# Moving the roundings, the bias and the rectifier of a feed-forward between ScalarE and VectorE

## The reference, cut to what matters

```python
q_mul = lambda x: _float_quantize(x, 5, 2)
q_acc = lambda x: _float_quantize(x, 5, 10)
def _qlinear(x, W, b):
    y = q_acc(jnp.einsum('bsk,nk->bsn', q_mul(x), q_mul(W)))
    return q_acc(y + q_mul(b))
h = jax.nn.relu(_qlinear(x, W1, b1))      # 96 -> 384
y = _qlinear(h, W2, b2)                   # 384 -> 96
# used as  t = t + ffn(layernorm(t))
```

## Time and profile before

| | |
|---|---|
| median of three executions | 7506.49 us |
| the profiled execution | 7508.82 us |
| its span in the profile | 7506.7 us |
| `ffn2`, from its first load's issue to that of the next phase | 6957.2 to 7128.1 us |
| `ffn3`, from its first load's issue to the end | 7335.3 to 7506.7 us |
| DVE, ACT, POOL busy over the whole span | 6432.9, 5446.9, 5465.7 us |

### The profile page before, as it was taken

How to read it: one execution, slowest core, us unless ns; L and a number is a source line. 1 busy time by engine, 2 the same in 40 slices (tenths; PEclk the granted TensorE clock), 3 DMA queues, 4 the chain that set the end, 5 groups by cost and what they waited for, 6 DMA issues and landing times. The chain is left out here.

```text
span 7506.7 us, 105881 instructions
## 1 busy us (share of the span) xinstructions
PE 6068.7 (81%) x18336; PEld 2113.4 (28%) x18336; DVE 6432.9 (86%) x7490; ACT 5446.9 (73%) x11128; POOL 5465.7 (73%) x4289
## 2 busy tenths in 40 slices
PE   7888888888888872888888888888887768798696
PEld 2222222222222220222222222222222113498252
DVE  6999999999999995499999999999999985533636
ACT  7888888888888873577777778777777764322757
POOL 5888888888888881488898898888888871000606
PEclk8999999889989986888999999999999888997898
DMA  4445445445445445587888888888877773346222
GB/s 101 108 104 117 107 106 116 107 108 115 106 106 116 106 101 143 115 186 182 186 187 185 187 189 186 185 188 187 187 183 186 184 165 92 124 137 195 81 57 77
DMA packets 584349, 1050.60 MB, mean 140 GB/s; under 512 B 105735, under 2 KB 140732, under 8 KB 579100
## 3 DMA queue, kind: packets, MB, share of 16 engines
q1 hardware_dynamic: 584060, 1047.70, 58.7%
HBM read 857.89 MB, written 189.54 MB: 140 GB/s over the span
## 5 line engine op out<-in xcount | busy, mean ns | idle before, releaser
L1644 POOL TENSOR_TENSOR scan_prod<-scan_hs,scan_BC_rep 128x512 f32<-128x512 f32 x1536 | 1943.8, 1273 | 312.8 <-DVE scan_hs L1568 303.8
L664 POOL TENSOR_TENSOR mamba_prod<-mamba_hs,mamba_BC_rep 128x512 f32<-128x512 f32 x1536 | 1919.7, 1274 | 216.6 <-DVE mamba_hs L621 214.8
L621 DVE TENSOR_TENSOR_SCAN mamba_hs<-mamba_dA,mamba_carry,mamba_dbx 128x512 f32<-128x512 f32 x1152 | 1425.3, 1265 | 1.6
L1193 PE MATMUL scan_u_rep<-scan_du,scan_sel 96*128 96x512 f32 x1536 | 935.2, 693 | 538.7 <-DVE scan_hs L1568 538.5
L546 ACT ACTIVATE mamba_dA<-mamba_delta_rep,mamba_a_neg 128x512 f32<-128x512 f32 x1536 | 1092.5, 712 | 121.5 <-DVE mamba_hs L621 118.8
L1418 ACT ACTIVATE scan_dA<-scan_delta_rep,scan_a_neg 128x512 f32<-128x512 f32 x1536 | 1092.3, 712 | 96.1 <-DVE scan_hs L1568 84.7
L1568 DVE TENSOR_TENSOR_SCAN scan_hs<-scan_dA,scan_carry,scan_dbx_even 128x512 f32<-128x512 f32 x768 | 975.8, 1271 | 45.6 <-ACT scan_carry L1398 27.9
L1568 DVE TENSOR_TENSOR_SCAN scan_hs<-scan_dA,scan_carry,scan_u_rep 128x512 f32<-128x512 f32 x768 | 976.3, 1271 | 40.8 <-ACT scan_carry L1398 36.7
L600 DVE TENSOR_TENSOR mamba_dbx<-mamba_u_rep,mamba_BC_rep 128x512 f32<-128x512 f32 x1152 | 776.7, 674 | 88.1 <-PE mamba_u_rep L332 75.6
L1967 POOL TENSOR_TENSOR ffn_sq<-ffn_xm 96x512 f32<-96x512 f32 x64 | 66.3, 1036 | 954.4 <-DVE ffn_xm L1935 943.3
L332 PE MATMUL mamba_u_rep<-mamba_du,mamba_sel 96*128 96x512 f32 x768 | 466.5, 692 | 317.4 <-DVE mamba_hs L621 316.9
(11 more groups left out here) (286 smaller groups left out, 10776.8 us busy)
## 6 DMA issues: line engine op xcount, KB each, us to landing
scan_BC_rep<-proj_rows SPq DMA_DIRECT2D x1024, 256.0 KB, 6.4
scan_delta_rep<-proj_rows SPq DMA_DIRECT2D x1024, 192.0 KB, 3.6
mamba_BC_rep<-bc_units SPq DMA_DIRECT2D x512, 256.0 KB, 8.1
mamba_delta_rep<-delta_units SPq DMA_DIRECT2D x512, 192.0 KB, 3.7
proj_rows<-scan_dbc SPq DMA_DIRECT2D x256, 224.0 KB, 3.4
delta_units<-mamba_delta SPq DMA_DIRECT2D x128, 192.0 KB, 5.8
by_n<-fin_res SPq DMA_DIRECT2D x32, 768.0 KB, 3.2
fmid_src<-by_n SPq DMA_DIRECT2D x32, 768.0 KB, 5.2
```

Source lines behind the costliest of these rows:

```text
L621: nc.vector.tensor_tensor_scan(hs[:, s % RING_H], dA[:, s % RING_A], dbx_bank(s)[:], carry[:, bass.ds(at, 1)], op0=ALU.mult, op1=ALU.add). ...
L664: pool.tensor_tensor(prod[:, (G * u + s) % RING_P], hs[:, s % RING_H], BC_rep[:, u, QUADS + s % QUADS], ALU.mult).then_inc(s_prod, 1)
L1193: nc.tensor.matmul(u_rep[c][:], sel[:, c], du[:, k], start=True, stop=True).then_inc(s_rep_u, 1)
L1644: pool.tensor_tensor(prod[:, (G * k + s) % RING_P], hs[:, (G * k + s) % RING_H], BC_rep[:, k, 2 + s % 2], ALU.mult).then_inc(s_prod, 1)
```

## The change

ScalarE's `relu` and `add_bias` go to VectorE, and VectorE's `round_sums` goes to ScalarE. ScalarE then reads both products out of PSUM; VectorE adds the biases, and the maximum with zero, with `tensor_scalar` from 16-bit SBUF tiles to 16-bit SBUF tiles. The wait for the bias tiles moves to VectorE with them. The lags stay; `relu` precedes `narrow` in VectorE's step, and `add_bias` is its last part.

```diff
-            def relu(n):
-                wait(act, s_h8, n - 1)
+            def round_sums(n):
                 for j in range(J):
-                    act.wait_ge(s_sum, J * n + j + 1)
-                    nc.scalar.activation(act16[:, n % 2, j], sum16[:, n % 2, j], ACT.Relu, bias=b1f[:, j:j + 1]
-                                         ).then_inc(s_act, 1)
+                    k = J * n + j
+                    act.wait_ge(s_hid, k + 1)
+                    wait(act, s_act, k - 2 * J + 1)
+                    nc.scalar.activation(sum16[:, n % 2, j], hid[k % HB][:], ACT.Copy).then_inc(s_sum, 1)
...
-            def add_bias(n):
-                act.wait_ge(s_o16, n + 1)
-                wait(act, s_res, n - 1)
-                nc.scalar.activation(y16[:, n % 2], out16[:, n % 2], ACT.Identity, bias=b2f[:]).then_inc(s_y16, 1)
-
             nc.scalar.preload_act_table_set(EXP_LN)
-            act.wait_ge(s_bq, 2)
             act.wait_ge(s_set, 2)
-            staggered(((4, log), (11, round_out), (5, rsqrt), (8, relu), (12, add_bias)))
+            staggered(((4, log), (11, round_out), (5, rsqrt), (7, round_sums)))
...
-            def round_sums(n):
+            def relu(n):
+                wait(dve, s_h8, n - 1)
                 for j in range(J):
-                    k = J * n + j
-                    dve.wait_ge(s_hid, k + 1)
-                    wait(dve, s_act, k - 2 * J + 1)
-                    nc.vector.tensor_copy(sum16[:, n % 2, j], hid[k % HB][:]).then_inc(s_sum, 1)
+                    dve.wait_ge(s_sum, J * n + j + 1)
+                    nc.vector.tensor_scalar(act16[:, n % 2, j], sum16[:, n % 2, j], b1f[:, j:j + 1], 0.0, ALU.add, ALU.max
+                                            ).then_inc(s_act, 1)
+
+            def add_bias(n):
+                dve.wait_ge(s_o16, n + 1)
+                wait(dve, s_res, n - 1)
+                nc.vector.tensor_scalar(y16[:, n % 2], out16[:, n % 2], b2f[:], None, ALU.add).then_inc(s_y16, 1)
...
-            staggered(((0, centre), (7, round_sums), (9, narrow)))
+            dve.wait_ge(s_bq, 2)
+            staggered(((0, centre), (8, relu), (9, narrow), (12, add_bias)))
```

## The result

The changed kernel takes 7540.49 us (median of 5 runs, 7532.7 to 7546.34) against 7502.77 for the kernel before (5 runs beside it, 7494.86 to 7511.48): a ratio of 1.0047, 95% interval 1.0034 to 1.006. The forecast was 7538 in a range of 7504 to 7571, slower by 31.6 us. The two medians differ by 37.7, the two profiled spans, 7544.5 and 7506.7, by 37.8.

The account below looks back on a forecast made before the run. POOL's 4.05 us middle step, its own work plus waiting in turns with VectorE's SBUF casts, was taken as the bound. 2 x (17.0 in the middle - 1.2 at the ends) = +31.6 us on 7506.5 gave 7538, range 7504 to 7571.

Parts of the forecast that it names:

- That the new instructions take turns: Feed-forward phases: VectorE's four new SBUF-to-SBUF instructions a unit alternate with POOL's, as the narrowing cast does; four turns more.
- The size of the step: Middle of both feed-forward phases: 4.90 us a step, the middle of two orders of turns, 0.85 over 4.05.
- order (a): Middle step: POOL, already waiting, wins after every VectorE instruction, and its next add waits for VectorE's bias; 4.94 us.
- order (b): Middle step: VectorE keeps its turn and POOL loses all five of VectorE's instructions in a row; 4.85 us.
- The add's new wait: Middle step: POOL's next add may start only after VectorE's bias, last in its step; included in 4.94 us.
- The number of middle steps: Middle of each phase: twenty steps, each 0.85 us longer, +17.0 us a phase.
- The filling: Four or five steps before unit 0's add in each phase: 0, with 1 us to either side.
- The ends: Last steps of each phase, without squares: 13.06 us become 11.84, a gain of 1.2 a phase; the last adds cancel.
- 1: Rival on the new VectorE instructions: they stream like 8-bit casts, 0.42 us each; +64 us, 7570 us; chance 0.13.
- 2: Rival on the new VectorE instructions: one element a cycle and no turns; +20 us, 7527 us; chance 0.08.
- 3: Rival: new instructions fast without turns, POOL keeps 4.05, ScalarE's relief shows at the ends; -14 us, 7493 us; chance 0.12.
- 4: Rival: TensorE's clock falls, a quarter of the 40 steps taking 7.0 us; 21 us more, 7559 us; chance 0.07.

Follow-up runs that it names:

- relu_psum: Kernel before with rectifiers on VectorE reading straight from PSUM, rounding of hidden sums left out, bias left on ScalarE: 7506.6 us against 7509.16, step 4.11.
- idle_psum: Changed kernel plus one useless VectorE cast of 256 columns out of PSUM per step, ahead of `centre`: 7569.23 us in one run, step 4.89.
- idle_sbuf: Changed kernel plus one useless VectorE copy of 512 columns between 16-bit SBUF tiles per step, behind `centre`: 7566.60 us in one run, step 5.16.
- bias_first: Changed kernel with the output's bias directly behind `centre` in VectorE's step: 7542.05 us in one run against 7515.94 for the kernel before, step 4.76.
- pe_order: Changed kernel with TensorE's hidden products issued ahead of the variance: 7564.25 us in one run beside 7524.40 for the kernel before, step 4.88.
- square_act_pe: Changed kernel with POOL's squares on ScalarE, a third x8 buffer and hidden products ahead of the variance: 7521.37 us in one run, step 4.21.
- square_act: Changed kernel with the square moved from POOL to ScalarE: 7514.0 us against 7509.16 for the kernel before, ratio 1.0007, step 4.09.
- relu_only: Changed kernel with the output's bias left on ScalarE, only the rectifiers on VectorE: 7531.88 us against 7509.16 for the kernel before, ratio 1.0032, step 4.56.

## Why the prediction was right

*The bound.* Right. The step was POOL's own work and its turns, and ScalarE's relief is worth nothing there: `relu_psum` gives it more relief and stands at 4.11.

*That the new instructions take turns.* Right, and the point on which the sign hung. `idle_psum` and `idle_sbuf` show it apart from load: +0.02 and +0.29 a step. Here the Trainium skill's rule ("SBUF — State Buffer", Who interferes with whom) holds for tensor_scalar and for a copy, both on 16-bit SBUF tiles; to the cast added from PSUM POOL lost 0.02 us a step, and in `relu_psum` two intervals of nineteen are left unexplained.

*The size of the step.* 4.90 forecast, 4.87 measured, but by two errors that cancel. I sized an instruction at 0.29; it takes 0.34, of which 0.06 is the bias operand. With 0.34 and the rest of my working unchanged, order (a) gives 4.94 + 4 x 0.05 = 5.14 and order (b) 4.85 + 4 x 0.05 = 5.05. Against it, I had a waiting VectorE instruction run its whole length after POOL's; it ends 0.15 us behind it (7063.56 behind 7063.41, 7067.01 behind 7066.86). So the bias costs the chain 0.15, where the sum with 0.34 has 0.33, and a POOL instruction that is let in after a single rectifier loses 0.05 (the square, 1.08 for 1.03), where that sum has 0.14. The order is neither (a) nor (b): POOL gets in after rectifiers 1 and 2 and after the cast, and `normalise` loses the rest of rectifier 2, rectifier 3 and the cast in one piece. A forecast as near as 0.03 us was luck, and so was the frame of 4.85 and 4.94; that four more turns lengthen the step well beyond 4.05 was the sound part of it.

*The add's new wait.* Right in kind, and priced in (a) without a figure of its own: it is 0.23 us of idleness, and 0.04 to 0.11 of the step by `bias_first`.

*The number of middle steps.* I took 20 steps, and there are 19 intervals between twenty adds: 15.5 us a phase, not 17.0.

*The filling.* The term that failed. I booked 0 with 1 us to either side; it measures +1.9 and +2.5. I had checked only a loop over three steps of 4.9 us; the trace shows a loop through the logarithm and the copies that closes within one step, 3.60 us, and holds from the first hidden products to the first add. `pe_order` opened it and gained nothing, as POOL's and VectorE's turns then hold the filling; the same reordering without POOL's squares, and with a third buffer for the 8-bit tile, brought the first add forward by 3.2 and 1.0 us (`square_act_pe` against `square_act`). In the kernels with parts of the change that keep POOL's squares the first add comes anywhere from 51.5 to 56.5 us; what sets this spread is open.

*The ends.* Forecast -1.2 a phase, measured -0.3 and +0.7. In `ffn2` the late adds are 3.83 us apart five times, then 2.81 three times, so the chain of ScalarE did give way as reckoned (2.96), by 0.8 us in all; the last four intervals, which I took to cancel, gave 0.8 back. In `ffn3` three of the earlier intervals are unequal (4.11, 4.73, 3.63), which costs 1.0 more. Sum: +31.6 forecast, +35.9 in the phases.

*ScalarE's idleness.* Forecast 1 to 1.8 us a step: 28.00 - 17.57 = 10.43 over 5.75 steps, 1.8.

*The rivals.* 1 (0.42 an instruction) and 2 (0.68, no turns) fall by the shortest record, 0.336. 3 (no turns) falls by the step; its second half, a gain at the ends, shows where the new turns are absent (`relu_psum`, 5 us a phase). 4 came half true: the granted clock did fall, to means of 0.86 and 0.77 in the windows above, where it was 1.00, and I had counted little on that. It cost the middle nothing: adds stay 4.87 apart through both windows. TensorE, busy for 23.19 to 24.53 of 28 us, has room for it, and what it then does late is waited for by nobody at the bound.

## What to carry to other kernels

Before moving work to an engine because another is full, ask which memory each moved instruction reads and writes, and whether GpSimd is at the bound: 0.34 us of VectorE on SBUF tiles cost more here than twice as much out of PSUM. Look for the shortest record of a line beside its median; here they differed by a factor of two and more because the engine waited inside its instructions, and its busy share of 100% said nothing of its load. If the relief of an engine off the bound is to pay, give it work from the bound in the same edit, and mind where the instruction that releases the bound's next one stands in its queue.

## What was unexpected of the hardware

- A VectorE instruction that waits for POOL's turn to end finishes 0.15 us after it, though alone it takes 0.34; so its first part seems to pass while it waits.
- Who gets the next turn is not fixed. With `normalise` waiting, VectorE ran the rest of one rectifier, another and the cast in a row, and `normalise` took 2.44 us; in `relu_only` the same POOL instruction takes 1.31, 2.44 and 1.28, in a pattern of three steps with adds 3.48, 4.15 and 6.19 us apart. What decides is open.
- A bias read per partition costs a 512-element VectorE instruction 0.06 us (336 against 276 ns).
- TensorE's granted clock fell from 1.00 to means of 0.86 and 0.77 in stretches in which TensorE ran fewer products than before (62 and 58 in 28 us, 71 before); in `square_act`, with 70, it was 1.00.
